# A transformer layer in one kernel: where the eighth tile of an expert group keeps its stationary operand

## The reference, cut to what matters

```
x + attention(xn) + ffn(xn)

attention: q, k = elu(.) + 1; kv = sum over k of k v; out = (q kv) / (q sum k), 16 heads, then Wo
ffn:   shared = swiglu(xn @ w_in.T) @ w_out.T
       h      = swiglu(xn @ w1.T)                        # 512 wide, the same for every expert
       routed = sum over the token's two best experts e of  weight[e] * (h @ w2[e].T)
```

## Time and profile before

| | before |
|---|---|
| median of three runs | 906.42 us (905.39 to 907.65) |
| the profiled execution, its own time | 906.74 us |
| its span | 904.8 us |
| TensorE busy | 887.8 us, 98% |
| VectorE busy | 692.0 us, 76% |
| GpSimd busy | 403.6 us, 45% |
| ScalarE busy | 367.3 us, 41% |
| mean granted clock of TensorE | 0.996 |
| expert stage, first to last matmul start | 687.8 to 895.9 us |

### The profile page before, as it was taken

How to read it: one execution, slowest core, us unless ns; L and a number is a source line. 1 busy time by engine, 2 the same in 40 slices (tenths; PEclk the granted TensorE clock), 3 DMA queues, 4 the chain that set the end, 5 groups by cost and what they waited for, 6 DMA issues and landing times. The chain is left out here.

```text
span 904.8 us, 22781 instructions
## 1 busy us (share of the span) xinstructions
PE 887.8 (98%) x6982; PEld 799.6 (88%) x6983; DVE 692.0 (76%) x1816; ACT 367.3 (41%) x605; POOL 403.6 (45%) x486
## 2 busy tenths in 40 slices
PE   8999999999999999999999999999998999999996
PEld 7798988889898989898888989898988999999996
DVE  6878778787878687877778786968684888777774
ACT  5654544353535445354435254554531222222220
POOL 4754342433334253434243342424332666656754
PEclk9999999999999999999999999999999999999999
DMA  6432414131323323141313232332145888888880
GB/s 219 138 118 71 128 47 128 70 104 70 104 93 105 108 89 110 64 128 49 125 70 104 77 109 86 100 126 72 59 185 132 144 148 146 146 142 144 150 150 1
DMA packets 141992, 98.63 MB, mean 109 GB/s; under 512 B 53136, under 2 KB 133008, under 8 KB 141968
## 3 DMA queue, kind: packets, MB, share of 16 engines
q1 hardware_dynamic: 103584, 62.50, 24.3%
q0 software_dynamic: 15920, 25.32, 12.3%
q10 hardware_dynamic: 22464, 10.51, 4.9%
HBM read 53.29 MB, written 46.43 MB: 110 GB/s over the span
## 5 line engine op out<-in xcount | busy, mean ns | idle before, releaser
L1239 POOL TENSOR_TENSOR h_lo<-gated,h_hi 128x256 fp32r<-128x256 f32 x128 | 98.7, 793 | 137.9 <-ACT h_hi L721 137.9
L362 PE MATMUL bank<-xnT_hi,win_hi 128*128 128x512 f32 x256 | 102.1, 399 | 0.0
L362 PE MATMUL bank<-wone_hi,xnT_hi 128*128 128x512 f32 x256 | 101.5, 397 | 0.2 <-DVE relut L1042 0.2
L363 PE MATMUL bank<-xnT_lo,win_hi 128*128 128x512 f32 x256 | 100.4, 392 | 0.0
L364 PE MATMUL bank<-wone_hi,xnT_lo 128*128 128x512 f32 x256 | 99.7, 390 | 0.0
L363 PE MATMUL bank<-wone_lo,xnT_hi 128*128 128x512 f32 x256 | 99.6, 389 | 0.0
L364 PE MATMUL bank<-xnT_hi,win_lo 128*128 128x512 f32 x256 | 99.6, 389 | 0.0
L1263 POOL TENSOR_TENSOR res<-res,bo_t 128x256 f32<-128x256 f32 x64 | 47.2, 769 | 111.3 <-DMA res<-x 111.3
L1258 POOL DMA_INDIRECT h_d<-hrow,pos_i x64 | 63.1, 986 | 73.1 <-DVE hrow L988 38.3
L362 PE MATMUL bank<-wexp_hi,xnT_hi 128*128 x304 | 84.5, 278 | 2.0 <-DVE xnT_lo L1161 2.0
L364 PE MATMUL bank<-wexp_hi,xnT_lo 128*128 x304 | 84.0, 276 | 0.0
(11 more groups left out here) (204 smaller groups left out, 2693.2 us busy)
## 6 DMA issues: line engine op xcount, KB each, us to landing
res<-x SPq DMA_DIRECT2D x16, 512.0 KB, 3.6
out<-res SPq DMA_DIRECT2D x16, 512.0 KB, 2.8
xt<-x SPq DMA_DIRECT2D x15, 512.0 KB, 3.4
xn_d<-xt SPq DMA_DIRECT2D x15, 512.0 KB, 4.9
xt<-xn_d SPq DMA_DIRECT2D x60, 128.0 KB, 2.7
xt<-h_d SPq DMA_DIRECT2D x76, 64.0 KB
xt<-h_d ACTq DMA_DIRECT2D x76, 64.0 KB
kb<-h_d SPq DMA_DIRECT2D x76, 64.0 KB
```

What stands on the lines that cost most here:

```text
L362: e.matmul(to, w_hi, m_hi_, start=first_, stop=False, skip_group_check=free)
L363: e.matmul(to, w_hi, m_lo_, start=False, stop=False, skip_group_check=free)
L1239: ins = pool.tensor_tensor(h_lo[j][:, cols], gated[:, j % 2, cols], h_hi[j][:, cols].bitcast(f32), ALU.subtract)
```

## The change

Only the first group's tile 7 keeps its place in `h0`. In all other groups tile 7 takes the place of tile 3, `h123` block 2, both for the high and for the low part. The tensors, their addresses, all waits and all counts are the same.

```diff
         def tile_parts(x, h):
             rows = [x[:, 0, :], x[:, 1, :], h[1], h[2]]
-            return [n.rearrange("p (j k) -> p j k", j=HC) for n in rows + rows[0:3] + [h[0]]]
+            return [n.rearrange("p (j k) -> p j k", j=HC) for n in rows + [h[0]]]
 
-        rh_hi, rh_lo = tile_parts(xnT_hi, h_hi), tile_parts(xnT_lo, h_lo)
+        parts_hi, parts_lo = tile_parts(xnT_hi, h_hi), tile_parts(xnT_lo, h_lo)
+
+        def place(t, g):
+            return TB if first_row(g) and t == GT - 1 else t % TB
+
+        def rh_hi(t, g):
+            return parts_hi[place(t, g)]
+
+        def rh_lo(t, g):
+            return parts_lo[place(t, g)]
...
-                            mm = mm3(pe, bank[t + n if apart else t][:, n * D:(n + 1) * D], rh_hi[t][:, j, :], rh_lo[t][:, j, :],
+                            mm = mm3(pe, bank[t + n if apart else t][:, n * D:(n + 1) * D], rh_hi(t, g)[:, j, :], rh_lo(t, g)[:, j, :],
...
-                act.copy(rh_hi[t], hT[t % 2]).then_inc(thi2, 1)
+                act.copy(rh_hi(t, g), hT[t % 2]).then_inc(thi2, 1)
...
-                dve.tensor_tensor(rh_lo[t], hT[t % 2], rh_hi[t].bitcast(f32), ALU.subtract).then_inc(tlo2, 1)
+                dve.tensor_tensor(rh_lo(t, g), hT[t % 2], rh_hi(t, g).bitcast(f32), ALU.subtract).then_inc(tlo2, 1)
```

## The result

The changed kernel is slower, not faster. Over 20 executions its median is 911.38 us (903.26 to 913.96), that of the kernel before 907.23 us (905.0 to 909.67); the ratio is 1.0031, 95% interval 1.0018 to 1.0043. The forecast was 905.1, in a range of 903.9 to 907.0.

The account below looks back on a forecast made before the run. TensorE, busy for 98% of the span and never waiting in groups 1 to 8, was taken as the bound. Eight tiles 7 at 0.16 us save 1.28, other terms zero: 906.42 - 1.28 = 905.14 us, range 903.9 to 907.0.

Parts of the forecast that it names:

- what tile 7 costs, and why: TensorE, groups 1 to 8: each tile 7 goes from 2.88 to 2.72 us by its operand's address, 1.28 us in all.
- The rival that the place does not matter: Tile 7: the 0.16 us belongs to bank 7 or the loop's jump, time stays 906.4 us; chance 0.05.
- reuse and writes: Tile 7's writes to another address, and sharing block 2 with tile 3: both taken as zero cost.
- step 4: TensorE's feeders in the expert loop: low parts stay early enough when TensorE speeds up 0.16 us per group; cost zero.
- the 2.72 us: TensorE, groups 1 to 8: time of each of tiles 0 to 6, expected to stay as it was.
- The sum: Whole kernel: 1.28 us off the profiled 906.74 gives 905.46; off the median 906.42 gives 905.14 us.
- something that I do not see: Leftover case for an effect not foreseen, with no size given; chance 0.02.
- The second rival: End of kernel: the table-row loader holds GpSimd back, time 907.0 or 906.3 us; chance 0.10, half each.

Follow-up runs that it names:

- before_load2: Kernel before, with TensorE's expert address load in tiles 2 and 6 instead of 0 and 4; ratio 0.9992, 11 executions from 905.36 to 908.71 us.
- after_again: The changed kernel run once more, unaltered, for a second profile; 906.67 us.
- after_load2: Changed kernel, with TensorE's expert address load in tiles 2 and 6 instead of 0 and 4; median 911.18 us, ratio 1.0027.
- tile3_320: Changed kernel, but in groups 1 to 9 tile 3 lies in h0 (320 modulo 512), tile 7 in h123 block 2; ratio 0.9994.
- half_320: Changed kernel, but tile 7 of groups 1 to 8 has blocks 2 and 3 in h0 (320 modulo 512), 0 and 1 in h123; ratio 0.9996.
- qn_320: Changed kernel, but tile 7 of groups 1 to 8 lies in qn, 320 bytes behind its start (320 modulo 512); ratio 0.9998.
- the straight code: TensorE's ten groups as straight code instead of a loop: changed kernel 914.17 us, ratio 1.0055; kernel before 914.37 us, ratio 1.0051.
- own_place: Changed kernel, but tile 7 of groups 1 to 9 lies in chunk 0 of qn (0 modulo 512), used by no other tile; median 907.22 us, ratio 1.0008.

## Why the prediction was wrong

**Right: what tile 7 costs, and why.** 0.16 us per tile by its address and not by its bank; the eight tiles are worth 183.40 - 182.13 = 1.27 us where the rhythm stays fast, against a forecast of 1.28. The rival that the place does not matter is out. The Trainium skill ("TensorE: Matmul & The Clock Gate", section "Back-to-back issue gap") gives its formula, an estimate of 109 ns for 256 columns, for a single matmul by itself, and for streams of load and matmul it gives other figures, at 128 and 512 columns. It has one spacing per column count; the runs show three for one shape at one clock, 113.3, 117.8 and 120 ns. The seven executions outside the high group have a median of 905.82 us, 1.4 below the 907.23 of before, as forecast; but a group that is picked by its times proves little.

**Right: reuse and writes cost nothing that the runs can show.** Tile 7 in a place of its own has the high group too, and the wait that opened the break in (2, 0) leads back to the loads of rows, not to a place in use.

**Wrong: step 4, "No feeder becomes late. Cost zero; bounds 0 and 0."** The step took a low part that is ready before its tile starts for early enough, and named just this tile: (2, 0), 2.20 us early. After, in the profiled execution, it was 0.61 us early, and that was too late, since the sequencer has to see it before it can hand over the tile. It was held 0.83 us, the register load then took 0.60 us, and the lead ran out. So the wait has to be measured against the sequencer, up to about 2.0 us ahead, and not against the matmul. That the change makes the rows late is not shown; they vary from one execution to the next, and `before_load2`, with tile 7 at 320, had a low part only 0.75 us early and kept the rhythm. In the kernel before, a break is paid for only up to the next tile 7 that restores the rhythm.

**Wrong beneath it: the 2.72 us were taken as a property of seven tiles.** They were a state, which tile 7 upheld. The sum subtracted tile 7's 0.16 us and left the others as they were. With a bad break in the middle of tile (2, 0), 58.5 tiles at 0.107 us more, and 0.09 for the break, make 6.3 us, and 6.3 less 1.3 is 5.0. The profiled execution's span grew by 5.5; 0.4 of the rest is that group 1 started later, at 712.90 in place of 712.49. The case falls under "something that I do not see", which had a chance of 0.02. The trace of before held the sign, in group 0, which I had left aside because the change does not touch it. First matmuls of (0, 5), (0, 6) and (0, 7):

```profile
703.97 0.28 PE L362 MATMUL bank<-wexp_hi,xnT_hi 128*128 x1
706.79 0.28 PE L362 MATMUL bank<-wexp_hi,h_hi 128*128 x1
709.62 0.28 PE L362 MATMUL bank<-wexp_hi,h_hi 128*128 x1
```

Two tiles at 0 modulo 512 with 2.82 and 2.83 us each, no wait in them, and 2.72 from 712.49 on the earlier trace rows, right behind the first tile at 320.

**The second rival was real, but not what decided.** The loader of the table rows cost 2.4 us at the end in the execution with a place of its own; in the two profiles of the changed kernel the last scatter waits for the sum.

**How sure the cause is.** In the 17 profiles, of before, after and the runs, I counted the expert stage's steps. No rhythm changed without a break (a step over 126 ns) or a tile at 320 or 64. Of 29 such tiles entered in the slow rhythm and left without a break, 26 left it fast; in the other three the steps went 120, 120, 125, 117, 118 over and over, and it stayed slow. Of 32 breaks out of the fast rhythm 27 ended slow, of some 85 out of the slow one 10 ended fast. The bound of 126 ns is a choice: the expectation of `after_again` had 124, the three tiles that stayed slow have steps of 124 and 125 without being counted as broken, and the break in `after_load2` is a single step of 127. That a tile at 320 in every loop round keeps the high group away rests on more than profiles: of the 44 executions of `before_load2`, `tile3_320`, `half_320` and `qn_320` none took 909 us. The three kernels without such a tile did in 13 of 20, 5 of 11 and 8 of 11. The kernel before did in 3 of 81 (909.1 to 910.0), and in 8 of the 14 beside the straight code (909.2 to 912.5), a set that lies higher as a whole; of it no profile was kept, so why is open. Open is what in the chip holds the rhythm, why the rows come later at one time than at another, and why `own_place` is in the high group less often than the changed kernel (5 of 11 against 13 of 20, which chance alone allows).

## What to carry to other kernels

An item that takes longer than its neighbours can be what keeps the neighbours fast; before removing it, look in the trace for the same work at another pace with no wait, and ask what ended that stretch. Read the steps between matmul starts, not the busy share: both rhythms read 98% busy. Where executions fall into two groups, compare profiles of both. An operand has to be early for the sequencer, not for the matmul: set the time at which it is ready against the sequencer's own records, and count register loads and jumps into the lead.

## What the runs showed of the hardware

- 128x128 stationary, 256 columns moving, fp32r, clock 1.00: 113.3 ns with the stationary operand at 0 or 256 modulo 512 bytes, 120 ns at 64 or 320, the moving operand at 320 in all. The Trainium skill's page "SBUF — State Buffer", section "Operand start alignment", says of its own runs that they are about legality, not speed, and timed nothing; here the start address has a price.
- After a break the spacing at 0 is 113.3 or 117.8 ns, and it kept the value for up to 67 tiles, to the end of the program.
- TensorE's sequencer is up to about 2.0 us ahead at a tile's first matmul. A jump back took it 0.6 us and a load of eight registers 0.59 to 1.02 us. A wait of 0.83 us for an operand showed as no idle time of TensorE, and still ended in a break.
- In the kernel with a wait in every group and tile 7 at 0, idle times of TensorE of about 2 us were in some groups followed by a stretch at a granted clock of 0.50, 1.2 GHz, for instance behind the break in front of tile (4, 2) (columns: window, its length, busy times of PE, PEld, DVE, ACT and POOL, then the clock, DMA share and rate):

```profile
799.10:801.00 1.90, 1.90 (x11) 1.90 (x10) 0.00 (x0) 0.00 (x0) 1.42 (x3) 0.50 0.81 149
```

  Matmul starts are 0.21 us apart there. In groups 1 to 8 of the kernels without this wait TensorE never stood that long.
